# A third sum in DRAM for the scattered expert rows of a recurrent block with a mixture of experts

## The reference, cut to what matters

```python
x = x + layernorm(attn(layernorm(x)))       # gates, a scan over the tokens, RMS norm, output product
x = x + layernorm(ffn(layernorm(x)))        # 16 experts, 4 for each token

# inside ffn, for x of 4096 tokens:
logits = x @ router_weight.T + router_bias
top_val, top_idx = top_k(logits, 4); top_val = softmax(top_val)
gate_up = einsum('th,ehd->etd', x, gate_up_proj) + gate_up_proj_bias     # 256 -> 2 * 256
glu = min(gate, 7) * sigmoid(1.702 * gate);  up = clip(up, -7, 7)
out = einsum('etd,edh->eth', (up + 1) * glu, down_proj) + down_proj_bias
out = (out * router_scores.T[:, :, None]).sum(axis=0)
```

## Time and profile before

| | |
|---|---|
| median of 3 runs | 800.43 us (793.66 to 808.1) |
| profiled execution, own time | 786.95 us |
| its span | 785.1 us |
| busy shares of the span | PE 84%, DVE 69%, ACT 59%, POOL 50% |
| DMA, mean over the span | 147 GB/s |

### The profile page before, as it was taken

The page is one execution under the profiler, slowest core; times in us unless marked ns, Lnnn a source line. Parts: engine busy times, 40 slices in busy tenths (PEclk is TensorE's granted clock), DMA queues, the critical chain, the costliest instruction groups (busy, mean ns, idle before and its releaser), DMA issues.

```text
span 785.1 us, 13641 instructions
## 1 busy us (share of the span) xinstructions
PE 657.3 (84%) x3818; PEld 424.8 (54%) x3818; DVE 540.5 (69%) x1595; ACT 461.0 (59%) x933; POOL 395.9 (50%) x300
## 2 busy tenths in 40 slices
PE   5988989599999846389799999999999999977450
PEld 2445646375665535246466666666666666644330
DVE  3626687768798877676477777777777776640992
ACT  2777786447567524235566777766777766650242
POOL 0012214754746626666666666666665656564111
PEclk9989998879999956579899999999999999995555
DMA  7966854699523212546677777777776766655987
GB/s 246 422 248 103 173 89 72 213 317 347 176 88 115 87 65 75 165 144 235 103 109 116 109 109 114 109 108 111 116 116 96 115 109 101 104 61 84 350 150 104
DMA packets 111897, 115.29 MB, mean 147 GB/s; under 512 B 31731, under 2 KB 101507, under 8 KB 110163
## 3 DMA queue, kind: packets, MB, share of 16 engines
q0 software_dynamic: 35456, 50.35, 38.0%
q1 hardware_dynamic: 76370, 64.07, 27.1%
HBM read 55.07 MB, written 59.31 MB: 146 GB/s over the span
## 4 chain that ended last, share of the span: by engine, by line
PE 45%; DMA 16%; DVE 15%; POOL 7%; issue 6%; ACT 6%; SPq 2%; POOLq 0%; ACTq 0%; DVEq 0%
DMA sums<-arena 10%; POOL routed L954 6%; PE PS L668 6%; PE PS L667 6%; PE PS L666 6%; PE PS L525 5%; PE PS L558 3%; PE PS L674 3%; PE PS L655 3%; PE PS L687 3%; PE PS L686 3%; PE PS L688 3%; PE PS L550 2%; ACT arena L740 2%; DMA W<-w_dn 2%
## 5 line engine op out<-in xcount | busy, mean ns | idle before, releaser
L980 POOL DMA_INDIRECT sums<-arena x144 | 222.8, 1547 | 127.2 <-DMA sums<-arena 61.1
L954 POOL DMA_INDIRECT routed<-arena,small x128 | 142.8, 1116 | 95.4 <-DVE small L1202 50.9
L1373 DVE TENSOR_SCALAR arena<-PS,small 128x256 f32<-128x256 f32 x144 | 78.4, 544 | 101.5 <-ACT arena L913 101.1
L525 PE MATMUL PS<-arena 128*128 128x512 f32 x256 | 127.5, 640 | 6.0 <-ACT arena L740 5.4
L740 ACT ACTIVATE arena<-PS 128x512 f16<-128x512 f16 (+1 forms) x180 | 105.3, 591 | 35.5 <-PE PS L566 15.0
L913 ACT ACTIVATE arena<-PS,small 128x256 f32<-128x256 f32 x144 | 68.2, 474 | 90.8 <-PE PS L668 90.4
L666 PE MATMUL PS<-W,arena 128*128 x288 | 111.2, 386 | 0.2 <-DVE arena L1375 0.2
L667 PE MATMUL PS<-W,arena 128*128 x288 | 111.1, 386 | 0.0
L668 PE MATMUL PS<-W,arena 128*128 x288 | 110.9, 385 | 0.0
L740 ACT ACTIVATE arena<-PS,arena 128x256 f32<-128x256 f32 x144 | 69.5, 483 | 33.6 <-DMA sums<-arena 29.4
L686 PE MATMUL PS<-W,arena 128*128 x288 | 79.1, 275 | 7.1 <-DVE arena L1363 5.7
(11 more groups left out here) (180 smaller groups left out, 1073.4 us busy)
## 6 DMA issues: line engine op xcount, KB each, us to landing
arena<-routed SPq DMA_DIRECT2D x144, 128.0 KB
W<-w_gu SPq DMA_DIRECT2D x8, 1024.0 KB, 23.4
W<-neg_mem POOLq DMA_DIRECT2D x16, 512.0 KB, 8.6
sums<-zero SPq DMA_DIRECT2D x2, 4096.0 KB, 26.1
W<-sums SPq DMA_DIRECT2D x16, 512.0 KB, 8.8
X<-x SPq DMA_DIRECT2D x8, 512.0 KB, 4.7
W<-w_dn SPq DMA_DIRECT2D x4, 1024.0 KB, 11.3
out<-X SPq DMA_DIRECT2D x8, 512.0 KB, 2.9
```

Source lines behind the costliest of these rows:

```text
L525: last = mm(PS[:, 2 + c % 2, :], WcT[:, k, c * P:(c + 1) * P], xT[:, k, :], start=(k == 0), stop=(k == KT - 1))
L954: pool.indirect_dma_start(routed, bass.IndirectOffsetOnAxis(ap=idx, axis=0), rows[b][:, jk // TOPK, :], None).then_inc(rows_sent[lane], 16)
L980: pool.indirect_dma_start(sums[j % SUMS], bass.IndirectOffsetOnAxis(ap=dst[j % MU], axis=0), yb[u], None, compute_op=ALU.add).then_inc(y_s ...
L1373: L.send(v.tensor_scalar(up[j % 2], acc[:, FF:2 * FF], gu_hi, gu_lo, ALU.min, ALU.max))
```

## The change

There are three sums. For tiles 0 to 95 scatter j goes to sum j mod 3 and waits for scatter j-3; from tile 96 on only sums 0 and 1 are used again, with a wait for scatter j-2 (from tile 98; tiles 96 and 97 still wait for 93 and 94). The third sum is zeroed like the others. SP loads it, 8 blocks of 512 KB, among the x and meta loads of tiles 112, 114, ..., 126. There are 12 result buffers in place of 8. There are 143 tiles, since 144 can't all be needed. POOL no longer waits for the landing of the rows of blocks 6 and 7 before it goes on. At the end a new DVE function `first(g)` computes `sum2 * y_inv + bias` for block g; the first three run ahead of the first `total`, the others two by two between the totals and the statistics of the pairs. ACT copies the router weights of five blocks ahead in place of four.

```diff
-TILES = -(-(ZROWS + E * (P - 1)) // P)
+TILES = (ZROWS + E * (P - 1)) // P
 UN = 8
+YU = 12
-SUMS = 2
+SUMS = 3
+SWITCH = 96
...
-        yb = [cut(DIM) for _ in range(UN)]
+        yb = [cut(DIM) for _ in range(YU)]
...
+        z3 = [cut(PART) for _ in range(NBLK - 3)]
+        z3 += [x2_own[:, :], W[:, PARTS_DN * PART:GU0 * PART], W[:, (SLOTS - 1) * PART:SLOTS * PART]]
...
                 if j >= MU:
-                    sp.wait_ge(y_sent[u], 16 * (j // UN - 1))
+                    sp.wait_ge(y_sent[(j - MU) % YU], 16 * ((j - MU) // YU + 1))
+                g, spare_turn = divmod(j - SWITCH - MU, 2)
+                if j == SWITCH + MU:
+                    sp.wait_ge(low_done, PARTS)
+                    sp.wait_ge(lo_ready, NBLK)
+                    for i in range(SWITCH - YU, SWITCH):
+                        sp.wait_ge(y_sent[i % YU], 16 * (i // YU + 1))
+                if 0 <= g < NBLK and not spare_turn:
+                    sp.dma_start(z3[g].rearrange("p (u d) -> p u d", u=BT),
+                                 sums[2][BLK * g:BLK * (g + 1), :].rearrange("(u p) d -> p u d", p=P)).then_inc(z3_in, 16)
                 sp.dma_start(meta[j % MU], pairs[ds(pairs_at[j], P, ROW // 2), :]).then_inc(meta_in[j % MU], 16)
...
-                    if t >= UN:
-                        act.wait_ge(y_sent[u], 16 * (t // UN))
+                    if t >= YU:
+                        act.wait_ge(y_sent[u], 16 * (t // YU))
...
-            for g in range(4):
+            for g in range(5):
                 evac_weights(g)
             for g in range(NBLK):
                 norm_z(g)
-                if g + 4 < NBLK:
-                    evac_weights(g + 4)
+                if g + 5 < NBLK:
+                    evac_weights(g + 5)
...
-                for lane in range(2):
-                    pool.wait_ge(rows_sent[lane], 16 * per * (t + 1))
-                pool.sem_inc(rows_free, 1)
+                if t + 2 < NBLK:
+                    for lane in range(2):
+                        pool.wait_ge(rows_sent[lane], 16 * per * (t + 1))
+                    pool.sem_inc(rows_free, 1)
...
-                if j >= SUMS:
-                    pool.wait_ge(y_sent[(j - SUMS) % UN], 16 * ((j - SUMS) // UN + 1))
-                pool.indirect_dma_start(sums[j % SUMS], bass.IndirectOffsetOnAxis(ap=dst[j % MU], axis=0),
+                last = j - (SUMS if j < SWITCH + 2 else 2)
+                if last >= 0:
+                    pool.wait_ge(y_sent[last % YU], 16 * (last // YU + 1))
+                pool.indirect_dma_start(sums[j % SUMS if j < SWITCH else j % 2], bass.IndirectOffsetOnAxis(ap=dst[j % MU], axis=0),
...
+            def first(g):
+                if g == 0:
+                    dve.wait_ge(z3_in, 16 * NBLK)
+                dve.wait_ge(bias_mm, g + 1)
+                v.scalar_tensor_tensor(z3[g], z3[g], y_inv, PS[:, 2 * (g % 3):2 * (g % 3) + 2, :].rearrange("p b x -> p (b x)"),
+                                       ALU.mult, ALU.add).then_inc(t_ready, 1)
+
             def total(g):
...
+                dve.wait_ge(t_ready, g + 1)
+                dve.wait_ge(blk_in[g], 32)
+                n = L.send(v.scalar_tensor_tensor(flat, flat, y_inv, z3[g], ALU.mult, ALU.add))
                 dve.wait_ge(z2_in[g], 16)
-                v.scalar_tensor_tensor(flat, flat2, y_inv, flat, ALU.mult, ALU.add).then_inc(t_ready, 1)
+                L.wait(n)
+                return L.send(v.scalar_tensor_tensor(flat, flat2, y_inv, flat, ALU.mult, ALU.add))
+
+            for g in range(3):
+                first(g)
 
             def two_groups(p):
                 for h in range(2):
-                    total(2 * p + h)
-                dve.wait_ge(t_ready, 2 * p + 2)
+                    n = total(2 * p + h)
+                for g in range(2 * p + 3, min(2 * p + 5, NBLK)):
+                    first(g)
+                L.wait(n)
```

More of the change, by code:

```diff
@@ L43 @@
 A_LAG, D_LAG = 3, 4
-TURNS = -(-TILES // UN)
-TILES = TURNS * UN
 HELD = 12
@@ L218, in build @@
         sg, act_ = [[cut(FF) for _ in range(NB)] for _ in range(2)]
-        yb = [cut(DIM) for _ in range(UN)]
+        yb = [cut(DIM) for _ in range(YU)]
         dst = [m[:, 0:1].bitcast(u32) for m in meta]
         wgt = [m[:, 1:2] for m in meta]
-        sT = [W[0:E, (SUMS * NBLK * PART + g * BLK):(SUMS * NBLK * PART + (g + 1) * BLK)] for g in range(NBLK)]
-        z, z2 = [[W[:, n * PART:(n + 1) * PART].rearrange("p (u d) -> p u d", u=BT) for n in range(a * NBLK, (a + 1) * NBLK)]
-                 for a in range(SUMS)]
+        sT = [W[0:E, (GU0 + NBLK) * PART + g * BLK:(GU0 + NBLK) * PART + (g + 1) * BLK] for g in range(NBLK)]
+        z, z2 = [[W[:, (at + n) * PART:(at + n + 1) * PART].rearrange("p (u d) -> p u d", u=BT) for n in range(NBLK)]
+                 for at in (0, GU0)]
+        z3 = [cut(PART) for _ in range(NBLK - 3)]
+        z3 += [x2_own[:, :], W[:, PARTS_DN * PART:GU0 * PART], W[:, (SLOTS - 1) * PART:SLOTS * PART]]
         sat = [0]
@@ L289, in build @@
         scale_ready, high_done, low_done = sem("scale_ready"), sem("high_done"), sem("low_done")
-        s_x = [sem(f"s_x{b}") for b in range(NBLK)]
+        blk_in = [sem(f"blk_in{b}") for b in range(NBLK)]
         nrow_in, nrow_ready, nrow_out, minus_done = sem("nrow_in"), sem("nrow_ready"), sem("nrow_out"), sem("minus_done")
@@ L320, in build @@
         y2_ready = sem("y2_ready")
-        y_sent = [sem(f"y_sent{u}") for u in range(UN)]
-        z_in = [sem(f"z_in{n}") for n in range(NBLK)]
+        y_sent = [sem(f"y_sent{u}") for u in range(YU)]
         z2_in = [sem(f"z2_in{n}") for n in range(NBLK)]
+        z3_in = sem("z3_in")
         zero_ready, zero_sent, x1_sent = sem("zero_ready"), sem("zero_sent"), sem("x1_sent")
@@ L482, in _ @@
                 if j >= MU:
-                    sp.wait_ge(y_sent[u], 16 * (j // UN - 1))
+                    sp.wait_ge(y_sent[(j - MU) % YU], 16 * ((j - MU) // YU + 1))
[8 more added lines that the diff above has]
+                                 sums[2][BLK * g:BLK * (g + 1), :].rearrange("(u p) d -> p u d", p=P)).then_inc(z3_in, 16)
                 sp.dma_start(meta[j % MU], pairs[ds(pairs_at[j], P, ROW // 2), :]).then_inc(meta_in[j % MU], 16)
-            for u in range(UN):
-                sp.wait_ge(y_sent[u], 16 * TURNS)
+            for u in range(YU):
+                sp.wait_ge(y_sent[u], 16 * len(range(u, TILES, YU)))
             for g in range(NBLK):
-                sp.dma_start(z[g], sums[0][BLK * g:BLK * (g + 1), :].rearrange("(u p) d -> p u d", p=P)).then_inc(z_in[g], 16)
+                sp.dma_start(z[g], sums[0][BLK * g:BLK * (g + 1), :].rearrange("(u p) d -> p u d", p=P)).then_inc(blk_in[g], 16)
                 sp.dma_start(z2[g], sums[1][BLK * g:BLK * (g + 1), :].rearrange("(u p) d -> p u d", p=P)).then_inc(z2_in[g], 16)
@@ L972, in _ @@
             for j in range(TILES):
-                u = j % UN
+                u = j % YU
                 pool.wait_ge(meta_in[j % MU], 16 * (j // MU + 1))
@@ L1021, in norms_x @@
                                        ALU.mult).then_inc(r1_ready, 1)
-            dve.wait_ge(s_x[0], 16)
+            dve.wait_ge(blk_in[0], 16)
             stats_x(0)
@@ L1037, in _ @@
             L(v.tensor_copy(dest, K[:, C_DEST:C_DEST + BT]))
-            dve.wait_ge(s_x[1], 16)
+            dve.wait_ge(blk_in[1], 16)
             stats_x(1)
@@ L1041, in _ @@
             for b in range(2, XRING):
-                dve.wait_ge(s_x[b], 16)
+                dve.wait_ge(blk_in[b], 16)
                 stats_x(b)
@@ L1314, in step @@
                 if ahead:
-                    dve.wait_ge(s_x[ahead], 16)
+                    dve.wait_ge(blk_in[ahead], 16)
                     stats_x(ahead)
```

9 lines of the change are left out of this document (2 added, 7 removed).

## The result

| | before | after |
|---|---|---|
| median | 797.04 us (788.65 to 808.1, 4 runs) | 813.57 us (810.83 to 820.84, 4 runs) |
| profiled execution, span | 785.1 us | 813.3 us |
| last scatter to the end | 66.3 us | 79.7 us |

The changed kernel is slower: ratio 1.0245, 95% interval [1.0194, 1.0297]. Each ratio in this text leaves out executions more than 1.5% above the fastest of the same kernel (here before's 808.1 us), so it isn't quite the quotient of the medians. The prediction (789 us, 770 to 808) was wrong in sign and outside its range.

What follows compares the result with a forecast made beforehand. POOL's scatters, only two out, lag PE's equal pace by five to six tiles. First total 709.6 + rest 58.7 + longer end 12.5 = 780.8 us span, 782.6 with surroundings; adjusted for the median's surplus, 789 us, range 770 to 808.

Steps and rivals of the forecast that it cites:

- This lag is born before tile 0: Start of tile stage: POOL, still busy with routed rows, scatters tile 0 at 372.75 us, when eight results wait.
- the last lines of the sum: Median lies 13.5 us above the profiled execution; if slower landings, 787 us, if elsewhere, 796; 789 taken.
- the gain of 16.8 us in front of the end: Ahead of DVE's first total: it starts at 709.6 us instead of 726.44; the end takes back 12.5 us.
- Block 6's waits: Routed rows on POOL: without the waits tile 0's scatter starts 4.15 us earlier, hidden unless the lag survives.
- Twelve buffers: Tile stage: PE and ACT no longer stop at tile 8; with 143 tiles the last copy ends 13.5 us earlier.
- Three sums: Scatters of tiles 0 to 95: at 1.85 us a scatter POOL has caught up with the copies at tile 33.
- The rival that it doesn't quicken POOL: Tile stage: DMA engines bound the scatters, the lag stays, last scatter at 720.2, time 801 us; chance 0.13.
- The loads of the third sum: Beside scatters 98 to 113: +1.0 us a landing, +8 us in all, between bounds of 0 and 40 us.
- The slower rival: Late tiles: landings reach 8.8 us beside the loads, last scatter at 734, time 815 us; chance 0.15.
- Third zero fill: Attention stage: about 12 us more of SP's queue, costing nothing, at most the part exceeding 10 us.
- The end: After the first total: late biases delay the pairs by 2.6, 7.3 and 2.6 us, +12.5 us in sum.
- Its own-time form: Whole kernel: predicted span 780.8 us against the profiled execution's 785.1, so -4.3 us, before adjusting for the median.

Runs made afterwards that it cites:

- b_again2: The kernel before, unchanged, run again on chip D: 810.49 us in its profiled execution; before's median there was 799.51 us.
- b_again: The kernel before, unchanged, run again on chip C: 784.46 us in its profiled execution, span 782.7 us.
- a_self: The changed kernel, unchanged, run again on chip C: 781.9 us against 783.85 us for the kernel before, ratio 1.0013.
- b_nowait6: The kernel before without POOL's waits behind the rows of blocks 6 and 7, on chip B: 803.48 us, ratio 1.0033.
- a_two: The changed kernel with every tile in sums 0 and 1, the third sum still zeroed, loaded and added, on chip C: 800.28 us, ratio 1.0128.
- b_zero3: The kernel before plus a third 4 MB zero fill into an unused tensor, on chip B: 801.94 us, ratio 1.0045.
- a_evac8b: The changed kernel with ACT copying all eight blocks' router weights before the first norm, a repeat on chip C: 773.65 us, ratio 0.9837.

## Why the prediction was wrong

**The step that failed** is the one ahead of all others: "This lag is born before tile 0", and with it the last lines of the sum, where the 13.5 us between before's profiled execution and its median were put down to slower landings. In the result scatter 0 starts 0.8 us after copy 0 has ended, not 18 or more, because copy 0 comes at 383.79 and not near 348. The trace that I read had no stall; the kernel before can have it, as `b_again2` shows. That its slower executions on the first chip had it is argued, from its 788 to 808 us there, which are like 788 to 811 on D, and not shown. On which chip before's profiled execution ran isn't on record. With the stall the tiles start late, all or most of POOL's rows are out when the first results come, and of the gain of 16.8 us in front of the end little or nothing is left.

**What the stall takes away.** From SP's first tile load to copy 8 all nine traces with the stall take 67.6 to 70.4 us, with two sums or three, with 8 buffers or 12. Without it `b_again` takes 52.3 and `a_self` 42.9. So the changed kernel gains 9.4 us in this stretch without the stall and none with it.

**In two sums.** Without it, on C, from the traces of `b_again` and `a_self`: copy 8 is 8.7 us earlier (361.07 for 369.74); from there to the last scatter it takes 331.5 in place of 345.9 us, -14.4; the end 79.5 in place of 67.0, +12.5. Together -10.6, and the spans differ by 10.6. With it, from `b_again2` and after: copy 8 to the last scatter 329.8 in place of 333.6 us, -3.9; the end 79.7 in place of 66.8, +12.9. Together +9.0 behind copy 8, by one trace of each kernel on different chips. The measured difference of the medians is 813.57 - 797.04 = 16.5 us (19.9 without before's 808.1). By this sum 7.5 us or more are left for the time ahead of copy 8, and no trace shows them. It may be that some executions of before had a shorter stall, or none, like its profiled one; the stalled trace of `b_again2` is before at its slowest. That the change itself lengthens the stall is not to be seen: copy 8 comes between 397 and 404 us in the five stalled traces with three sums, and between 395 and 411 in the four with two. Whether the change makes the stall more frequent stays open.

**Block 6's waits.** Predicted: hidden unless the lag survives. `b_nowait6`: 1.0033, nothing.

**Twelve buffers.** Predicted: no stop at tile 8, last copy 13.5 us earlier. On C the stop is gone and the last copy of `a_self` is at 681.98, that of `b_again` at 700.55: -18.6, of which 2.4 is the tile less and about 8 the stop. In `b_again` copies 16 to 96 come 2.436 us apart and not 2.400, so there the full buffers hold ACT (24.1 us of waits for scatters between 400 and 580 us, none of note in before's trace), which the sum didn't have. Right there, worth nothing with the stall.

**Three sums.** Predicted: POOL level by tile 33. In `a_self` the lag falls from 20.6 us at tile 0 to 10.9 at tile 16 and is 0.7 to 1.4 us from tile 36 on. The rival that it doesn't quicken POOL fell with `a_two`: 18.4 us slower than `a_self` on the same chip, where before's medians in the two groups differ by 2.8.

**The loads of the third sum.** I took +1.0 us a landing and +8 us in all between bounds of 0 and 40. Measured: +0.9 us a landing, and the last scatter 5.4 to 7.8 us later. What was missed is small: POOL falls behind from tile 96 on, 4.8 us by the end without any load, where 2.5 were predicted. The slower rival, landings of 8.8 us, has the right sign by the wrong mechanism; that its 815 us are near the 813.57 is luck. The Trainium skill ("DMA: Bandwidth & Descriptors", section Queues, rings and completion order) says that a DMA engine goes round its queues a packet at a time. The landings agree with that: +0.9 us, where even sharing of the 1.13 us of a scatter's packets would give about that much more.

**Third zero fill.** Predicted at nothing; `b_zero3` measured 0.45% (about 4 us), not clear of nothing, and copy 0 of `a_self` (341.01) is where that of `b_again` is (340.97).

**The end.** Predicted +12.5 us; measured +12.5 on C, +13.4 in the result. It went by the steps that the prediction gave. DVE's second pair, and PE's biases of blocks 5 and 6:

```profile
755.96 1.28 DVE L1410 SCALAR_TENSOR_TENSOR W<-W,small,arena 128x1024 f32<-128x1024 f32 x1
...
762.49 1.28 DVE L1403 SCALAR_TENSOR_TENSOR x_own<-x_own,small,PS 128x1024 f32<-128x1024 f32 x1 [1.27 <-PE PS L733]
...
767.15 1.28 DVE L1403 SCALAR_TENSOR_TENSOR W<-W,small,PS 128x1024 f32<-128x1024 f32 x1 [3.38 <-PE PS L733]
768.35 2.71 DVE L1426 BATCH_NORM_STATS2 small<-W 128x6 f32<-128x256 f32 x8
```

```profile
758.68 3.77 PE L733 MATMUL PS<-Bdn,W 16*128 16x256 f32 x8 [12.98 <-ACT W L750]
763.33 3.78 PE L733 MATMUL PS<-Bdn,W 16*128 16x256 f32 x8
```

The statistics come 12.39 us after the pair begins (predicted 12.44), behind waits of 1.27 and 3.38 us (predicted 1.3 and 3.4). PE had stood for 12.98 us, waiting for ACT's copy, which waits behind a norm. With all eight copies ahead of the norms (`a_evac8b`) the biases are done early and the same pair takes 721.97 - 714.41 = 7.56 us:

```profile
707.93 7.19 PE L733 MATMUL PS<-Bdn,W 16*128 16x256 f32 x16
```

```profile
714.41 1.28 DVE L1408 SCALAR_TENSOR_TENSOR W<-W,small,arena 128x1024 f32<-128x1024 f32 x1
...
720.78 1.27 DVE L1401 SCALAR_TENSOR_TENSOR W<-W,small,PS 128x1024 f32<-128x1024 f32 x1
721.97 2.71 DVE L1424 BATCH_NORM_STATS2 small<-W 128x6 f32<-128x256 f32 x8
```

**The sum.** Its own-time form, -4.3 us, is near what chip C measured: medians of 781.9 and 783.85. The two profiled executions there differ by more (-10.6); `a_self`'s, 773.95 us, is the lowest of its ten. What made the other executions of `a_self` 8 us longer isn't known. In the traces the gain in front of the end is 23 us and not 16.8, in the medians about 14: that the sum comes out near the medians of C is no proof of its terms.

## What to carry to other kernels

A gain that consists in catching up is worth what there is to catch up with. Ask which executions have the lag, and when the profiled one is faster than every timed run, take the surplus for something that this trace doesn't show, perhaps in just the stretch that the argument rests on. A second profile of before, on another chip too, would have shown it here. What a change adds behind the last dependency (here 12.5 to 13.4 us) was paid in every trace, what it recovers only in some. Where a step of the end wants more operands at once, move their producers ahead of the engine's consumer work: that was an edit of a few lines, and worth 6 to 8 us.

## What the runs showed of the hardware

- Chips differ by nearly as much as this change: the kernel before took 784 to 789 us (medians) on C and E and 798 to 800 on B and D. On B and D all eight profiled executions have the stall; on C and E none of the ten. Of the first two profiles, read for the prediction and the result, before's has none and after's has it.
- In the stall PE, DVE and ACT stop for up to 11 us, often with nothing late that the profile shows, and some of SP's register instructions, which move no data, take 0.7 us, while POOL issues indirect row DMAs 1.28 us apart and the DMA engines are at 0.27 to 0.51. SP's steps begin in after 5.5 us after its first tile load (333.45 to 338.99), but DVE's holes are there from 204 us on: in each of the nine traces with the stall they add up to 3.5 to 10.4 us ahead of the first tile load, in each of the eleven others to 0.5. So the tile loads aren't all that sets it off. What does is open: it isn't the 8-byte loads, and it needs no part of the change, since the kernel before has it too.
- A scatter beside 512 KB loads lands in 4.8 us in place of 3.9, far from the 8.8 that such loads take when they fill the engines.
